# A cross-attention and expert-FFN kernel: branch behind the masks, narrowing of the pivots divided anew, part of the low weight halves on VectorE

## What is computed

```python
Q, K = ctx @ Wq.T, ctx @ Wk.T                      # heads are summed, so sim is one Q @ K.T
sim = Q @ K.T / (sqrt(16) * 4)                     # 256 x 256 per batch
A = sigmoid(sim) * (sim >= 76th largest of its row)
A = (A + A.T) / 2
x1 = x + (1 - g) * layernorm(x) + g * A            # g = sigmoid(gamma_raw)
z = layernorm(x1)
scores = softmax(z @ gate_w.T); comb = scores at the 2 best of 8 experts, else 0
y = sum_e comb[:, e] * ((silu(z @ w1[e].T) * (z @ w3[e].T)) @ w2[e].T)
out = x1 + y + (silu(z @ ws1.T) * (z @ ws3.T)) @ ws2.T
```

## Time and profile before

| | us |
|---|---|
| median of 3 runs (lowest, highest) | 121.78 (120.93, 122.46) |
| the profiled execution | 122.4 |
| its span | 120.6 |
| TensorE busy (share of the span) | 105.2 (87%) |
| weight loads of TensorE busy | 101.4 (84%) |
| VectorE busy | 83.1 (69%) |
| ScalarE busy | 55.0 (46%) |
| GpSimd busy | 84.3 (70%) |

### The profile page before, as it was taken

How to read it: one execution, slowest core, us unless ns; L and a number is a source line. 1 busy time by engine, 2 the same in 40 slices (tenths; PEclk the granted TensorE clock), 3 DMA queues, 4 the chain that set the end, 5 groups by cost and what they waited for, 6 DMA issues and landing times.

```text
span 120.6 us, 2390 instructions
## 1 busy us (share of the span) xinstructions
PE 105.2 (87%) x790; PEld 101.4 (84%) x790; DVE 83.1 (69%) x265; ACT 55.0 (46%) x128; POOL 84.3 (70%) x137
## 2 busy tenths in 40 slices
PE   6996082259999999999999999999989999999991
PEld 6775072158899989999999999999979999999990
DVE  6578996984695998769939896965555770708632
ACT  4149989299708612361768412104093243224310
POOL 4037878895799988999998899962827675075800
PEclk9999855555899999999999999999999999999999
DMA  2899992000000017000045000020441100902002
GB/s 55 206 297 297 323 369 79 0 5 3 0 5 0 0 44 313 0 3 0 0 130 226 0 0 0 8 90 0 163 185 43 49 0 3 345 8 90 0 0 87
DMA packets 7069, 10.32 MB, mean 86 GB/s; under 512 B 1360, under 2 KB 5968, under 8 KB 6544
## 3 DMA queue, kind: packets, MB, share of 16 engines
q1 hardware_dynamic: 6688, 10.13, 24.9%
q10 hardware_dynamic: 368, 0.04, 0.2%
HBM read 9.09 MB, written 1.08 MB: 84 GB/s over the span
## 4 chain that ended last, share of the span: by engine, by line
PE 75%; DVE 8%; ACT 5%; POOL 4%; issue 3%; DMA 2%; DVEq 1%; ACTq 0%; POOLq 0%; SPq 0%
PE ps_h L1248 21%; PE ps_u L1248 20%; PE ps_y L1276 16%; PE ps_u L1141 4%; PE ps_a L1276 3%; PE ps_c L1216 3%; PE ps_a L1176 2%; DMA weights<-gates 2%; PE ps_b L1199 2%; PE ps_h L1165 1%; DVE left L849 1%; POOL gc L423 1%; DVE near L855 1%; ACT qkT L551 1%; DVE g_lo L1001 1%
## 5 line engine op out<-in xcount | busy, mean ns | idle before, releaser
L423 POOL TENSOR_TENSOR gc<-prod,weights 128x512 f32<-128x512 f32 x16 | 25.5, 1609 | 13.3 <-DMA weights<-gates 7.4
L634 ACT ACTIVATE sil<-ps_h 128x512 f32<-128x512 f32 (+1 forms) x20 | 10.8, 549 | 25.1 <-PE ps_h L1248 24.8
L1001 DVE TENSOR_TENSOR g_lo<-gc,g_hi 128x512 fp32r<-128x512 f32 x16 | 13.3, 841 | 11.4 <-ACT g_hi L645 11.2
L1276 PE MATMUL ps_y<-dn_hi,g_hi 128*128 128x256 f32 x63 | 18.2, 289 | 0.5 <-DVE g_lo L1001 0.5
L1276 PE MATMUL ps_y<-dn_lo,g_hi 128*128 128x256 f32 x63 | 17.8, 282 | 0.0
L1276 PE MATMUL ps_y<-dn_hi,g_lo 128*128 128x256 f32 x63 | 17.8, 282 | 0.0
L645 ACT ACTIVATE g_hi<-gc 128x512 fp32r<-128x512 f32 x16 | 9.7, 625 | 13.8 <-POOL gc L423 13.8
L1248 PE MATMUL ps_h<-z_hi,up_hi 128*128 128x256 f32 x72 | 15.0, 289 | 0.3 <-issue 0.3
L1248 PE MATMUL ps_h<-z_lo,up_hi 128*128 128x256 f32 x72 | 14.5, 282 | 0.0
L1248 PE MATMUL ps_h<-z_hi,up_lo 128*128 128x256 f32 x72 | 14.4, 281 | 0.0
L1248 PE MATMUL ps_u<-z_hi,up_hi 128*128 128x256 f32 x72 | 14.4, 281 | 0.0
(11 more groups left out here) (173 smaller groups left out, 253.0 us busy)
## 6 DMA issues: line engine op xcount, KB each, us to landing
weights<-gates SPq DMA_DIRECT2D x4, 1024.0 KB, 4.5
x_sb<-in_x SPq DMA_DIRECT2D x4, 256.0 KB, 5.9
up_raw<-in_w1t SPq DMA_DIRECT2D x4, 256.0 KB, 6.4
up_raw<-in_w3t SPq DMA_DIRECT2D x4, 256.0 KB, 6.6
dn_raw<-in_w2t SPq DMA_DIRECT2D x4, 256.0 KB, 7.2
out_x<-fin SPq DMA_DIRECT2D x3, 256.0 KB, 2.4
out_x<-fin SPq DMA_DIRECT2D x2, 128.0 KB, 1.7
ctx_sb<-in_ctxT SPq DMA_DIRECT2D x1, 192.0 KB, 4.4
```

The lines of the kernel that those rows point to most:

```text
L423: nc.gpsimd.tensor_tensor(gc[k % 2][:, :].rearrange("p (n t q) -> p n t q", n=2, t=T), prod[s][:, :].rearrange("p (n t q) -> p n t q", n=2 ...
L634: nc.scalar.activation(sil[i % 2][:, :w], ps_h[i % 2][:, :w], ACT.Silu).then_inc(silu_ready, 1)
L1001: nc.vector.tensor_tensor(g_lo[s][:, :], src[:, :], g_hi[s][:, :].bitcast(F32), ALU.subtract).then_inc(glo0_ready if s == 0 else glo_ready, 1)
L1276: last = nc.tensor.matmul(dst[:, t * D:(t + 1) * D], g[s][:, tok], w[:, e, :], start=(s == 0 and first and m == 0), stop=(s == SLOTS - 1 a ...
```

## The change

- *Late branch.* `select(b)` takes the place of `check_hits`, `pick_kth` and `mask`: picks, then the load of the register, then masks, then the branch. The slow search now repeats picks and masks inside the branch. A memset behind it sets `checked`, for which `transpose_masked` and `add_masked` wait.
- *Narrowing of batch 0, divided.* VectorE narrows tile 0 (`aims0`, `narrow0`, `count_last0`), ScalarE tile 1 with Sign sums (`lean_first`, `lean_second`, `lean_last`); each next pivot is one multiply and add with numbers that GpSimd prepares (`make_spans`, `spans0`). The last count is VectorE's.
- *Narrowing of batches 1 to 3.* ScalarE works out the pivots itself, by Identity with scale and bias of one column per tile; GpSimd only prepares their factors (`steps(b)`, for `first_pivot`); `second_pivot` and `third_pivot` are gone.
- *Low halves.* `lower_up` of slots 1 and 3 (four of ten, each 128x512) is VectorE's.
- *Routing.* The power on GpSimd is replaced by Tanh(d/2) on ScalarE and three VectorE operations, (1 + t) / (1 - t). comb and weights are stored in two halves, each with a load of 512 KB and a semaphore of its own.
- *Order.* All five orders are written anew. Those of the head:
  - VectorE: zero_rows, copy_k0, first_score_stats, norm1 0, aims0, norm1 1, narrow0 0, gamma_parts, narrow0 1, count_last0 0 and 1, drop_above 0, take_near 0 (both), read_hits 0, select 0, add_masked0, lower_up(1,0), residual1 0, lower_up(1,1), count_above 1, norm2_first, drop_above 1, take_near 1 (both), read_hits 1, low_z 0, select 1, score_stats 2, route_a 0, gate_values(0,0), residual1 1, low_g(0,0), route_b 0, gate_values(0,1), lower_up(3,0), lower_up(3,1), norm1 2, low_z 1 and so on.
  - ScalarE: copy_q0, tanh_first, copy_qk 1, copy_qk 2, tanh_gamma, lean_first, copy_qk 3, upper_gate, lean_second, upper_up(0,0), lean_last, copy_scores_summed, sigmoid 0, upper_down 0, normed1 0, sigmoid 1, upper_up(0,1), (1,0), (1,1), first_balance 1, second_balance 1, last_pivot 1, upper_up(2,0), (2,1), copy_scores 2, upper_down 1, upper_up(3,0), high_z 0, copy_scores 3, normed1 1 and so on.
  - GpSimd: make_ones, make_spans, make_halves, make_ident, deviation0, make_ranks, spans0, norm1 0, lower_up(0,0), find_hits 0, steps 1, lower_down 0, norm1 1, lower_gate, norm2 0, make_routing_consts, find_hits 1, lower_up(0,1), (2,0), (2,1), add_masked 1, steps 2, norm2 1, lower_up(4,0), (4,1) and so on.
  - TensorE: keep_warm 5, project 0, keep_warm 1, similar 0, keep_warm 1, project 1 and 2, keep_warm 1, project 3, keep_warm 7, similar 1, similar 2, keep_warm 5, sum_hits 0, keep_warm 2, transpose_masked 0, keep_warm 1, similar 3, keep_warm 7, sum_hits 1, keep_warm 1, transpose_z 0, keep_warm 4, up(0,0), logits 0, keep_warm 1, transpose_masked 1, up(0,1), up(0,2), down(0,0), transpose_z 1, up(0,3), logits 1 and so on.

```diff
+STEP = 0.5 / DENSITY
+STEP2 = STEP * SECOND_STEP
+BIAS = float(N - 2 * AIM)
...
+VECTOR_LOWERED = (1, 3)
...
-                sp.dma_start(gates[b], comb[:, :, :]).then_inc(gates_out, 16)
+                sp.dma_start(gates[b].rearrange("i p t e -> p i t e"), comb[:, :, :, :]).then_inc(gates_out, 16)
                 sp.wait_ge(gates_out, 16 * (b + 1))
                 if b >= 1:
                     sp.wait_ge(gc_ready, gated(b - 1, SLOTS - 1))
-                sp.dma_start(weights[:, :], gates[b].rearrange("p t e -> (p t e)").partition_broadcast(P))\
-                    .then_inc(weights_in, 16)
+                for i in range(2):
+                    sp.dma_start(weights[i][:, :], gates[b][i].rearrange("p t e -> (p t e)").partition_broadcast(P))\
+                        .then_inc(weights_in[i], 16)
...
+                nc.gpsimd.tensor_tensor(dev[0][:, :], mv0[0][:, :, 1], plus_half[:, :], ALU.pow).then_inc(dev0_ready, 1)
+
+            def spans0():
+
+                pool.wait_ge(dev0_ready, 1)
+                nc.gpsimd.tensor_tensor(step_a[:, :], dev[0][:, :], scale_a[:, :], ALU.mult)
+                nc.gpsimd.tensor_tensor(step_b[:, :], dev[0][:, :], scale_b[:, :], ALU.mult)
+                nc.gpsimd.tensor_tensor(shifted_a[:, :], dev[0][:, :], shift_a[:, :], ALU.mult)
+                link(nc.gpsimd.tensor_tensor(shifted_b[:, :], dev[0][:, :], shift_b[:, :], ALU.mult))
+                nc.gpsimd.tensor_tensor(from_a[:, :], shifted_a[:, :], mv0[0][:, :, 0], ALU.add)
+                nc.gpsimd.tensor_tensor(from_b[:, :], shifted_b[:, :], mv0[0][:, :, 0], ALU.add).then_inc(span_ready, 1)
...
+            def steps(b):
+
+                if b == 1:
+                    pool.wait_ge(sums_ready, 1)
+                    link(nc.gpsimd.tensor_scalar(mean1[:, :], score_sum[:, :], 1.0 / N, None, ALU.mult))
+                    link(nc.gpsimd.tensor_tensor(mean_sq[:, :], mean1[:, :], mean1[:, :], ALU.mult))
+                    link(nc.gpsimd.tensor_tensor(var0[b][:, :], score_sq[:, :], mean_sq[:, :], ALU.subtract))
+                    var, mean = var0[b][:, :], mean1[:, :]
+                else:
+                    pool.wait_ge(stats0_ready, b)
+                    var, mean = mv0[b][:, :, 1], mv0[b][:, :, 0]
+                link(nc.gpsimd.tensor_tensor(dev[b][:, :], var, plus_half[:, :], ALU.pow))
+                for i, k in enumerate((-FIRST_PIVOT, -FIRST_PIVOT - STEP * BIAS, FIRST_PIVOT + (STEP + STEP2) * BIAS)):
+                    nc.gpsimd.tensor_scalar(offset[b][i][:, :], dev[b][:, :], k, None, ALU.mult).then_inc(pool_self, 1)
+                    done[0] += 1
+                for k, dst in ((STEP, step[b]), (-STEP, neg_step[b]), (STEP2, step2[b])):
+                    nc.gpsimd.tensor_scalar(dst[:, :], dev[b][:, :], k, None, ALU.mult)
+                pool.wait_ge(pool_self, done[0])
+                for i, (dst, op) in enumerate(((neg_pivot[b][0], ALU.subtract), (neg_base[b], ALU.subtract),
+                                               (pivot_base[b], ALU.add))):
+                    last = nc.gpsimd.tensor_tensor(dst[:, :], offset[b][i][:, :], mean, op)
+                last.then_inc(pivot0_ready, 1)
 
...
             def second_balance(b):
...
+                for t in range(T):
+                    act.wait_ge(balance0_ready, T * (b - 1) + t + 1)
+                    nc.scalar.activation(neg_pivot[b][1][:, t:t + 1], balance[b][0][:, t:t + 1], ACT.Identity,
+                                         bias=neg_base[b][:, t:t + 1], scale=neg_step[b][:, t:t + 1])\
+                        .then_inc(pivot1_ready, 1)
+                    nc.scalar.activation(pivot_part[b][:, t:t + 1], balance[b][0][:, t:t + 1], ACT.Identity,
+                                         bias=pivot_base[b][:, t:t + 1], scale=step[b][:, t:t + 1])\
+                        .then_inc(part_ready, 1)
+                for t in range(T):
+                    act.wait_ge(pivot1_ready, T * (b - 1) + t + 1)
+                    nc.scalar.activation(sides[1][t][:, :], scores[b][:, t, :], ACT.Sign,
+                                         bias=neg_pivot[b][1][:, t:t + 1],
+                                         accum_out=balance[b][1][:, t:t + 1]).then_inc(balance1_ready, 1)
...
+            def last_pivot(b):
+
+                for t in range(T):
+                    act.wait_ge(balance1_ready, T * (b - 1) + t + 1)
+                    act.wait_ge(part_ready, T * (b - 1) + t + 1)
+                    last = nc.scalar.activation(pivot[b][:, t:t + 1], balance[b][1][:, t:t + 1], ACT.Identity,
+                                                bias=pivot_part[b][:, t:t + 1], scale=step2[b][:, t:t + 1])
+                last.then_inc(pivot_ready, 1)
...
+            def lean_second():
+
+                act.wait_ge(lean_ready, 1)
+                act.wait_ge(span_ready, 1)
+                nc.scalar.activation(aim1[:, 1:2], lean[:, 0:1], ACT.Identity, bias=from_a[:, 1:2],
+                                     scale=step_a[:, 1:2]).then_inc(lean_aim_ready, 1)
+                nc.scalar.activation(part0[:, 1:2], lean[:, 0:1], ACT.Identity, bias=from_b[:, 1:2],
+                                     scale=step_a[:, 1:2]).then_inc(lean_part_ready, 1)
+                act.wait_ge(lean_aim_ready, 1)
+                nc.scalar.activation(lean_sides[1][:, :], ps_first[1][:, 0:N], ACT.Sign, bias=aim1[:, 1:2], scale=-1.0,
+                                     accum_out=lean[:, 1:2]).then_inc(lean_ready, 1)
...
+            def tanh_logits(b):
+                act.wait_ge(lgd_ready, b + 1)
+                if b >= 1:
+                    act.wait_ge(exp_ready, b)
+                nc.scalar.activation(th[:, :, :], lgd[:, :, :], ACT.Tanh, scale=0.5).then_inc(th_ready, 1)
...
+            def lower_up(s, a):
+
+                e = slice(experts_of(s)[0], experts_of(s)[-1] + 1)
+                dve.wait_ge(up_hi_ready, 2 * s + a + 1)
+                nc.vector.tensor_tensor(up_lo[:, e, a], up_raw[:, e, a], up_hi[:, e, a].bitcast(F32),
+                                        ALU.subtract).then_inc(vector_lo_ready, 1)
...
+            def count_first(t, at):
+                return nc.vector.tensor_scalar(over[:, t, :], scores_of(0, t), at[:, t:t + 1], 0.0,
+                                               ALU.is_gt, ALU.add, accum_out=count[:, t:t + 1])
+
+            def narrow0(i):
+
+                if i == 0:
+                    dve.wait_ge(aim_ready, 1)
+                    dve.wait_ge(tanh_ready, 1)
+                    link(count_first(0, aim0))
+                    dve.wait_ge(span_ready, 1)
+                    nc.vector.tensor_scalar(part0[:, 0:1], count[:, 0:1], step_a[:, 0:1], from_b[:, 0:1],
+                                            ALU.mult, ALU.add)
+                    link(nc.vector.tensor_scalar(aim1[:, 0:1], count[:, 0:1], step_a[:, 0:1], from_a[:, 0:1],
+                                                 ALU.mult, ALU.add))
+                else:
+                    link(count_first(0, aim1))
+                    link(nc.vector.tensor_scalar(pivot[0][:, 0:1], count[:, 0:1], step_b[:, 0:1], part0[:, 0:1],
+                                                 ALU.mult, ALU.add))
+
+            def count_last0(t):
+
+                if t == 1:
+                    dve.wait_ge(lean_pivot_ready, 1)
+                last = count_first(t, pivot[0])
+                if t == 1:
+                    last.then_inc(count_ready, 1)
...
+            def select(b):
 
                 if b == 0:
                     dve.wait_ge(above_ready, 1)
                 for t in range(T):
                     dve.wait_ge(dve_self, near_mark[t])
+                    last = pick_kth(t)
                 last.then_inc(kth_ready, 1)
                 dve.wait_ge(hits_taken, b + 1)
                 all_hits = dve.value_load(hits[0:1, 0:1], min_val=0, max_val=N)
+                dve.wait_ge(kth_ready, b + 1)
+                dve.wait_ge(sig_ready, b + 1)
+                for t in range(T):
+                    mask(b, t).then_inc(masked_ready, 1)
                 with dve.If(all_hits < N):
                     n = 0
...
+                nc.vector.memset(looked[:, :], 0.0).then_inc(checked, 1)
...
+                dve.wait_ge(th_ready, b + 1)
+                link(nc.vector.tensor_scalar(th_below[:, :, :], th[:, :, :], -1.0, 1.0, ALU.mult, ALU.add))
+                link(nc.vector.reciprocal(th_below[:, :, :], th_below[:, :, :]))
+                nc.vector.scalar_tensor_tensor(ex[:, :, :], th[:, :, :], 1.0, th_below[:, :, :],
+                                               ALU.add, ALU.mult).then_inc(exp_ready, 1)
...
                     pe.wait_ge(masked_ready, T * b + t + 1)
+                    pe.wait_ge(checked, b + 1)
```

459 lines of the change are left out of this document (234 added, 225 removed).

## The result

| | before | after |
|---|---|---|
| median (lowest, highest), us | 122.09 (120.93, 122.46) | 115.88 (115.10, 116.47) |
| profiled execution, its span | 122.4, 120.6 | 115.1, 113.3 |
| TensorE, VectorE, ScalarE, GpSimd busy | 105.2, 83.1, 55.0, 84.3 | 104.7, 85.7, 62.5, 70.4 |

The change makes the kernel faster: ratio 0.953, 95% interval 0.948 to 0.958. The median of before is of four executions here, three of which gave the 121.78 from which the prediction starts. The profiled execution of before was its slowest and that of after its fastest, so the two spans differ by 7.3 us and the medians by 6.2.

A forecast was written before the change was run, and what follows sets the result against it. TensorE's dense stream of expert matmuls was taken as the bound, so its start decides: 121.78 before, minus 5.3 for an earlier start, plus 0.6 given back in the stream, gives 117.1 us, range 115.4 to 120.0.

The forecast's parts named there:

- 1, narrowing divided: Head, batch 0: tile 0 counted on VectorE, tile 1 on ScalarE; last count ends at 13.2 instead of 14.2, gain 1.0 us.
- 3, late branch: Branch after each batch's picks and masks: halts of about 1 us shrink, gain 0.7 us per batch, at worst 0.
- 4 and 5, the residual: VectorE, head: batch 0's residual ahead of batch 1's count and top-8; gains summed to 5.5, walked 6.0, statistics end at 20.6.
- 6 and 7, z and the start: Head: z of batch 0 at 22.8, up(0,0) about 26.2, up(0,1) 29.5 instead of 34.78, 5.3 us gained.
- the prediction's last paragraph: List of signs for and against, wrong if TensorE waits for VectorE's prod or z waits for batch 1's pivot.
- 8, the work moved between engines: Low halves to VectorE, powers to ScalarE's tanh: GpSimd loses over 20 us, none on the path once the stream runs.
- held-up reads: VectorE reading two SBUF tensors beside running GpSimd: 0.7 us more per lower_up, 1.0 per ex.
- The stream: Expert matmuls on TensorE starting 5.3 us earlier: VectorE's extra work gives back 0.6 us, between nothing and 2.1.
- E: Extra work on VectorE during the expert matmuls, 5.4 us, set against 3.3 us of idle time left.
- the clock fell in the head: Rival, chance 0.17: TensorE's clock falls in shorter gaps of the head, +1.6 us, 118.7.
- VectorE gives part back: Rival, chance 0.12: VectorE's extra work stays at 5.4 us, time 119.2.
- VectorE becomes the bound: Rival, chance 0.06: from 27 to 76 us VectorE's extra work reaches 13.4, +4.8 us, 126.6; slower from 8.6 on.

The follow-up runs named there:

- narrow_vector: Changed kernel with batch 0's narrowing on VectorE alone, both tiles, ScalarE's five operations for tile 1 removed: 116.65 us, ratio 0.960.
- early_branch: Changed kernel with load, compare and branch again ahead of picks and masks: 117.9 us, ratio 0.973.
- residual_late: Changed kernel with batch 0's residual and norm2_first back behind batch 1's count, drop and top-8: 124.15 us, ratio 1.025.
- b_residual: Kernel before with only add_masked0 and residual1(0) moved ahead of count_above(1): 122.02 us, ratio 1.004.
- vector_extra: Changed kernel with five more 128x512 operations on VectorE, results unused, 3.4 us of work: 121.06 us, ratio 0.994.
- fewer_warm: Changed kernel with ten warm-up matmuls instead of 27 between project(3) and up(0,0): 117.1 us, ratio 0.966.

## Why the prediction was right, and where not

It said 117.1 us (115.4 to 120.0), and faster. The medians are 115.88 and 116.74. Its steps, in order:

- *1, narrowing divided.* The last count of batch 0 was foreseen to end at 13.2; it ends at 12.35, which with the A of before is 13.24. Right for the place, but for what it is worth the step held too much: narrow_vector shows at most 0.65 of 1.0. A small Identity takes 0.37 to 0.39 us at a spacing of 0.28, not 0.2 to 0.25.
- *3, late branch.* 0.7 per batch foreseen; in batch 0 the idle time went from 0.92 to 0.69 only, but the picks (0.4) moved ahead of it; early_branch prices all of it at 0.9 us of start and 1.2 to 2.0 of time. Halts under 0.4 us held for batches 1 to 3 (0, 0.28, 0) and not for batch 0.
- *4 and 5, the residual.* End of the statistics at 20.6 foreseen, at 20.23 measured (21.12 with the A of before): right within 0.5. residual_late and b_residual show what the step did not say: the move is worth 7 to 8 us with the rest of the order laid out for it and nothing without it.
- *6 and 7, z and the start.* z at 22.8, up(0,0) at 26.2, up(0,1) at 29.5 foreseen; 23.16, 26.42 and 29.87 with the A of before. 5.3 us gained foreseen, 4.9 measured. ScalarE's queue held z by way of batch 1's count, as the step said; the prediction's last paragraph had the same wait down as a sign of being wrong, as it had any wait of TensorE for prod, of which there is one of 0.37 us at 42.99.
- *8, the work moved between engines.* Here a step failed. "None of it is on the path once the stream runs" was wrong for GpSimd's powers: putting them back into the new order costs 6.3 to 7.1 us, since find_hits(2) stands behind the gates there. The account of GpSimd's relief should have asked what waits for comb. GpSimd's busy time fell by 13.9 us (84.3 to 70.4), not by over 20; the new small operations (`steps(b)`, `spans0`) were left out of that count. Of the new operations of VectorE, the four lower_up took 0.67 or 0.68 us each, and ex 0.17 or 0.18 in three batches and 1.42 in the last: of the 0.7 and 1.0 us for held-up reads that the prediction set against the change, one was paid, at 89.82. Nothing shows a gain from weights in two halves: each landed in a median of 4.8 us, no earlier than the whole. GpSimd waited 9.2 us for them instead of 7.4, without a wait of TensorE behind it in after.
- *The stream.* 0.6 us given back was foreseen; nothing was. From up(0,1) to VectorE's last residual it is 81.78 us long in after and 82.51 when run again, before 83.28, so 0.8 to 1.5 shorter. TensorE's waits in it are 0.37 us in after, 0.86 when run again and 0.76 in before, so they explain 0.4 of it at most. The matmuls of `down` are 0.4 to 2% shorter, and why is open. VectorE is busy 0.8 us more over 47.02 us from up(0,1) on (37.59 to 38.41), not the 5.4 of E. But the rule by which 0.6 was made, idle time less extra work, is refuted by vector_extra: 3.4 us in places with 8.6 idle cost 4.3 to 5.2.

So the forecast is borne out by its start. Its start gains 0.4 us too much and its stream is 1.4 to 2.1 too long, and it lies 1.2 and 0.4 us above the two medians. That the 0.6 did no more harm was luck, as the rule behind it doesn't hold.

Of the rivals, the clock fell in the head (0.50 over 17.00 to 20.00) but was at 1.00 from 24.00 on; fewer_warm shows up(0,1) 2.15 us later with fewer warm-ups. The price of "VectorE gives part back" is added up wrongly: 121.78 - 5.3 + 2.1 is 118.6, and 119.2 counts the 0.6 twice. "VectorE becomes the bound" did not happen, but lies nearer than 0.06 and "from E = 8.6 on" made it: one 1.96 us operation in the wrong place is enough.
